# Four of sixteen state drives made with tokens on partitions by ScalarE and turned by TensorE

## Chip, cores and metric
The kernel runs on one core of one Trainium2 chip. The metric is the device time of one execution in microseconds (us), the median of several runs.

## The reference
The input is `x` (4 images, 64 channels, 32x32 positions; so 4 sequences of 1024 tokens). First comes a Mamba block in two directions over the tokens, forward and backward. For one direction and one image, with 128 inner channels and 16 states:

```
xp, z = x @ W_in                       # 128 channels each
xc    = silu(xprev * conv_w0 + xp * conv_w1 + conv_b)
dt_r, Bc, Cc = xc @ W_x                # 8, 16 and 16 columns
dt    = softplus(dt_r @ W_dt + b_dt)
h_s   = exp(dt * A_s) * h_s + (dt * xc) * B_s       # per state s, over the tokens
y     = sum over s of h_s * C_s  +  D * xc
out   = (y * silu(z)) @ W_out
```

The two directions are added, a group norm with silu and the input follow, then causal attention over the tokens and a spectral expert layer. The change touches the Mamba block alone.

## The kernel before
The Mamba stage handles 8 units, u = 0 to 7: image b = u // 2, direction i = u % 2 (0 forward, 1 backward). A tensor of a unit is 128 channels on partitions by 1024 tokens, float32. Every unit goes through its 16 states s in order. The first image is written out, the middle two are a hardware loop, the last is written out. Each engine has its own queue in program order, and semaphores join them.

For a state, four things are made:
- a decay, `exp(dt * A_s)`, by ScalarE (`decay_of`, L734), two states ahead, into one of three SBUF buffers. For states 2, 3, 6, 9, 15 it goes to PSUM instead (`shared_decay_of`, L740): 3, 6, 9 (`WIDE_SHARED`) into `ps_w`, 2 and 15 into `ps_d`;
- a drive, `dtx * B_s`, where `dtx = dt * xc`. B_s is one row of 1024 numbers, spread by a DMA over all 128 partitions into one of four `b_wide` buffers. VectorE makes it into `ps_d` (`drive_step`, L874) for eleven states; GpSimd makes it into SBUF (`share`, L445) for 2, 3, 6, 9, 15, up to three states ahead;
- the scan over the tokens, by VectorE (`scan_step`, L888), into one of four `hidden` buffers;
- the product with C_s by GpSimd (`prod`, L455), and its sum over states in PSUM `ps_y` by TensorE (`sum_states`, L551), three states behind (`Y_LAG`).

In between, the engines prepare the next unit v, in `ps_w`. TensorE: the gate projection (`gate_in`, at s = 2), the conv projection (`conv_in`, s = 3), the low-rank projection (`low_rank`), `dt_in` at s = 10, and matmuls with a unit matrix that add up softplus (`add_rectified`, `add_exponential`, `add_logarithm`). ScalarE: `take_z`, `silu_gate`, `silu_input`, `take_low`, the softplus functions, `take_dt`, `keep_dtx`. `ps_w` passes in turn between these and the decays of states 3, 6 and 9: the decay of 6 waits for `silu_input`, for instance. VectorE makes `dtx` of the next unit in PSUM `ps_x` after scan 14 (`dt_x`, L862), and the gated output of the unit before after scan 1 (`gate_of`, L869). At s = 3 of a forward unit TensorE makes the out product of the image before (`out_product`) and ScalarE takes it (`norm_take`); at s = 3 of a backward unit VectorE ends the group norm's columns and ScalarE applies them (`norm_silu`). `D * xc` is a matmul of `xc` with a diagonal matrix that starts each unit's sum in `ps_y` (`skip_in`, L545).

The SyncE queue issues the B and C loads of each state in turn, each once the buffer's last user is done. In the last unit only state 6 is GpSimd's, and pieces of the attention stage are worked in.

Of the kernel before, what the change touches and what calls it, by code (L numbers as in the profile page):

```python
# [22 lines left out]
ALU = mybir.AluOpType  # L23
# [3 lines left out]
B = 4  # L27
# [5 lines left out]
R = 8  # L33
# [25 lines left out]
POOL_STATES = (2, 3, 6, 9, 15)  # L59
WIDE_SHARED = POOL_STATES[1:4]  # L60
DRIVE_OF = {2: 0, 3: 1, 6: 0, 9: 1, 15: 0}
SHARE = len(POOL_STATES)
SHARE_AHEAD = 3
# [146 lines left out]
def mamba_stage(nc, ins, a, g, e, x1):  # L210
# [6 lines left out]
    with ExitStack() as ctx:  # L217
# [3 lines left out]
        def sem(name):  # L221
# [20 lines left out]
        xc = [sb(f"xc_{d}", [D, L]) for d in DIRS]  # L242
# [7 lines left out]
        rectified = sb("rectified", [D, L])  # L250
        minus_ident = sb("minus_ident", [128, 128])
        skip = [sb(f"skip_{d}", [D, D]) for d in DIRS]
# [5 lines left out]
        b_wide = [sb(f"b_wide_{i}", [D, L]) for i in range(BC_DEEP)]  # L258
# [18 lines left out]
            out_ready a_log_ready one_plus_ready minus_one_ready dt_summed share_ready share_decay diag_ready minus_ready z_kept sum_step tok_psum tok_ready ln_step ln_rstd xn_ready  # L277
# [5 lines left out]
         gated_ready, out_ready, a_log_ready, one_plus_ready, minus_one_ready, dt_summed, share_ready, share_decay, diag_ready, minus_ready, z_kept, sum_step,  # L283
# [5 lines left out]
        b_in = [sem(f"b_in_{i}") for i in range(BC_DEEP)]  # L289
# [8 lines left out]
        LAST_SHARE = POOL_STATES[2:3]  # L298
# [3 lines left out]

        def driven_before(u, s, last=False):
            return (N - SHARE) * u + s - sum(p < s for p in shared(last))

        def shared_before(u, s, last=False):
            return SHARE * u + sum(p < s for p in shared(last))

# [16 lines left out]
        with nc.Block() as block:  # L325

            @block.sync
            def _(sp):
# [39 lines left out]

                def spread(wide, row, done):
                    sp.dma_start(wide[:, :], bass.AP(bc_rows.tensor, row * L, [[0, 128], [1, L]])).then_inc(done, 16)  # L370

                def spread_b(u, i, s):
                    if u or s >= BC_DEEP:
                        drive_done(*divmod(u * N + s - BC_DEEP, N))
                    spread(b_wide[s % BC_DEEP], i * 2 * N + s, b_in[s % BC_DEEP])
# [5 lines left out]
                def unit(u, i):  # L381
                    sp.wait_ge(bc_out, 16 * (u + 1))
                    for s in range(N):
                        spread_b(u, i, s)
# [17 lines left out]
            def _(pool):  # L402
# [38 lines left out]
                def share(u, s):  # L441

                    pool.wait_ge(dtx_kept, u + 1)
                    pool.wait_ge(b_in[s % BC_DEEP], 16 * (u * (N // BC_DEEP) + s // BC_DEEP + 1))
                    nc.gpsimd.tensor_tensor(drive[DRIVE_OF[s]][:, :], dtx[:, :], b_wide[s % BC_DEEP][:, :], ALU.mult).then_inc(share_ready, 1)  # L445

                def batch(b, first=False, last=False):
                    for i in range(2):
                        u = 2 * b + i
                        for s in range(N):  # L450
# [6 lines left out]
                            if s + SHARE_AHEAD in shared(last and i == 1):  # L457
                                share(u, s + SHARE_AHEAD)
                            if s + SHARE_AHEAD - N in shared(last and i == 0) and not (last and i == 1):
                                share(u + 1, s + SHARE_AHEAD - N)  # L460
# [15 lines left out]
                share(0, POOL_STATES[0])  # L476
# [6 lines left out]
            def _(pe):  # L483
# [9 lines left out]
                def gate_in(u, i, b):  # L493

                    pe.wait_ge(dtx_ready, u)
# [8 lines left out]
                def low_rank(u, i):  # L504

                    pe.wait_ge(xc_ready, u + 1)
                    for h, out in enumerate(halves(ps_w)):
                        mm = nc.tensor.matmul(out[0:DT_ROW + R, :], w_x[i], halves(xc[i])[h], start=True, stop=True)
# [9 lines left out]
                def add_part(w, part, start=False, stop=False):  # L518
                    for h, out in enumerate(halves(ps_w)):
                        mm = nc.tensor.matmul(out, w[:, :], halves(part)[h], start=start, stop=stop)  # L520
                    return mm

                def add_rectified(u):

                    pe.wait_ge(abs_ready, u + 1)
                    pe.wait_ge(relu_ready, u)
                    add_part(ident, rectified, start=True)

                def add_exponential(u):

                    pe.wait_ge(exp_ready, u + 2)
                    add_part(ident, soft)

                def add_logarithm(u, i):
# [4 lines left out]
                    add_part(ident, dt[i], stop=True).then_inc(dt_summed, 1)  # L539

                def skip_in(u, i):

                    at_least(pe, gated_ready, u)
# [1561 lines left out]
```

## Time and profile before

| | |
|---|---|
| median of 3 runs | 949.73 us (949.38 to 951.89) |
| span of the profiled execution | 947.3 us |
| from that span to the median | 2.4 us |
| TensorE busy, whole span | 834.3 us, 88% |
| VectorE busy | 710.7 us, 75% |
| GpSimd busy | 549.2 us, 58% |
| ScalarE busy | 508.3 us, 54% |

The profile is one execution. Its span runs from the first to the last instruction; the profiled execution's own time outside the profiler is not listed, so the median stands beside it. Busy shares are over the whole span, though the stages differ: the Mamba stage ends near 482 us, attention near 640 us, and the expert stage, in which TensorE is the busiest, takes the rest. Engines are called PE (TensorE), PEld (its weight loads), DVE (VectorE), ACT (ScalarE), POOL (GpSimd), SP (SyncE).

### The profile page before, as it was taken

What the parts mean: (1) busy time and instruction counts of PE and PEld (TensorE: products, weight loads), DVE (VectorE), ACT (ScalarE), POOL (GpSimd) and SP (SyncE); (2) the same over time, 40 slices, a digit from 0 to 9 for tenths busy, and PEclk for the clock granted to TensorE, in tenths of its full rate; (3) what the DMA queues carried; (4) which work ended last, traced back from release to release, by engine and by line L of the source; (5) the groups of instructions that cost most, each with busy time, mean ns of one, the idle gap of its engine ahead of it and who ended that gap; (6) DMA issues with size and microseconds to landing.
All of it is one profiled execution on the core that took longest, in us unless ns stands there. A gap on an engine that the chain in (4) does not pass through costs nothing. (4 is left out here: it accounts for less than half of the span.)

```text
span 947.3 us, 10224 instructions
## 1 busy us (share of the span) xinstructions
PE 834.3 (88%) x3004; PEld 492.0 (52%) x3004; DVE 710.7 (75%) x767; ACT 508.3 (54%) x702; POOL 549.2 (58%) x373
## 2 busy tenths in 40 slices
PE   5579897979899898986687999989999999999996
PEld 1224342433334333332243555558888888888885
DVE  1999999999999999999965455546565665565664
ACT  4645666556566666643315446456555554555553
POOL 4678989999998998875736955312212211212210
PEclk9799999999999999997987999999999999999999
DMA  7969898889879898796609800002343342343341
GB/s 167 342 201 344 312 332 273 337 311 305 324 257 369 308 327 309 279 328 222 202 0 137 157 0 1 1 1 63 117 133 100 122 133 90 90 133 100 122 118 59
DMA packets 75349, 178.24 MB, mean 188 GB/s; under 512 B 24514, under 2 KB 25044, under 8 KB 75300
## 3 DMA queue, kind: packets, MB, share of 16 engines
q1 hardware_dynamic: 75316, 177.85, 57.9%
q8 instruction: 14, 0.23, 0.1%
q14 instruction: 19, 0.16, 0.1%
HBM read 175.57 MB, written 2.26 MB: 188 GB/s over the span
## 5 line engine op out<-in xcount | busy, mean ns | idle before, releaser
L455 POOL TENSOR_TENSOR prod<-hidden,c_wide 128x1024 f32<-128x1024 f32 x128 | 300.0, 2356 | 64.6 <-DVE hidden L888 60.5
L551 PE MATMUL ps_y<-prod,ident 128*128 128x512 f32 x512 | 244.2, 622 | 27.9 <-POOL prod L455 27.7
L888 DVE TENSOR_TENSOR_SCAN hidden<-decay,ps_d 128x1024 f32<-128x1024 f32 x92 | 209.9, 2281 | 8.3
L1920 PE MATMUL ps_conv<-hankel,u_high 128*128 128x512 f32 (+1 forms) x768 | 215.3, 361 | 0.0
L551 PEld LDWEIGHTS ps_y<-prod,ident 128*128 128x128 f32 x512 | 99.0, 198 | 169.2 <-issue 116.7
L1920 PEld LDWEIGHTS ps_conv<-hankel,u_high 128*128 128x128 f32 x768 | 138.6, 189 | 25.4 <-DVE u_t L1786 0.2
L1920 PE MATMUL ps_conv<-hankel,u_low 128*128 128x512 f32 (+1 forms) x384 | 138.1, 360 | 0.0
L2034 DVE TENSOR_TENSOR stack<-ps_conv,stack 64x512 fp32r<-64x512 f32 x128 | 88.2, 689 | 62.7 <-ACT stack L2001 60.2
L1751 POOL CAST block_mix<-even 128x256 fp32r (+1 forms) x32 | 12.7, 396 | 209.3 <-PE sums L1792 209.3
L2034 DVE TENSOR_TENSOR qk<-ps_conv,qk 64x512 fp32r<-64x512 f32 x128 | 88.2, 689 | 50.2 <-ACT qk L2001 47.5
L874 DVE TENSOR_TENSOR ps_d<-ps_x,b_wide 128x1024 f32<-128x1024 f32 x92 | 113.3, 1232 | 4.9 <-DMA b_wide<-bc_rows 0.4
L2001 ACT ACTIVATE stack<-ps_conv 64x512 fp32r<-64x512 f32 x128 | 75.9, 593 | 75.0 <-PE ps_conv L1920 73.1
L2001 ACT ACTIVATE qk<-ps_conv 64x512 fp32r<-64x512 f32 x128 | 75.9, 593 | 63.3 <-PE ps_conv L1920 61.3
L445 POOL TENSOR_TENSOR drive<-dtx,b_wide 128x1024 f32<-128x1024 f32 x36 | 84.9, 2357 | 6.4 <-ACT dtx L729 6.4
L1920 PEld LDWEIGHTS ps_conv<-hankel,u_low 128*128 128x128 f32 x384 | 72.8, 190 | 13.8
L734 ACT ACTIVATE decay<-dt_b,a_neg_b 128x1024 f32<-128x1024 f32 x48 | 53.2, 1140 | 35.9 <-DVE hidden L888 35.5
L888 DVE TENSOR_TENSOR_SCAN hidden<-ps_w,drive 128x1024 f32<-128x1024 f32 x22 | 50.1, 2279 | 0.0
L734 ACT ACTIVATE decay<-dt_f,a_neg_f 128x1024 f32<-128x1024 f32 x44 | 48.2, 1137 | 2.0 <-DVE dt_f L852 0.9
L1472 DVE TENSOR_REDUCE max_parts<-sums 128x1 f32<-128x512 f32 (+1 forms) x48 | 27.4, 597 | 24.8 <-PE sums L1147 15.2
L1060 POOL TENSOR_TENSOR small<-small,minus_half 128x8 f32<-128x8 f32 x4 | 6.6, 1644 | 55.0 <-DVE small L1442 55.0
L1340 ACT ACTIVATE probs<-ps_t 128x512 f32<-128x512 f32 (+1 forms) x48 | 24.8, 521 | 22.6 <-PE ps_o L1192 22.2
L1792 PE MATMUL sums<-stack,block_mix 128*128 128x512 f32 (+1 forms) x160 | 32.5, 349 | 2.1 <-DVE stack L2034 2.1
(283 smaller groups left out, 1158.8 us busy)
## 6 DMA issues: line engine op xcount, KB each, us to landing
b_wide<-bc_rows SPq DMA_DIRECT2D x128, 512.0 KB, 5.6
c_wide<-bc_rows SPq DMA_DIRECT2D x128, 512.0 KB, 5.2
hankel<-filters SPq DMA_DIRECT2D x32, 1026.0 KB, 5.2
plus<-in_M_phi_plus SPq DMA_DIRECT2D x2, 1024.0 KB, 13.5
minus<-in_M_phi_minus SPq DMA_DIRECT2D x2, 1024.0 KB, 18.9
x_pair<-in_x SPq DMA_DIRECT2D x2, 768.0 KB, 8.5
bc_rows<-mixed_and_low SPq DMA_DIRECT2D x8, 128.0 KB, 5.4
out<-plus SPq DMA_DIRECT2D x4, 256.0 KB, 4.9
```

The source lines that it names most:

```text
L445: nc.gpsimd.tensor_tensor(drive[DRIVE_OF[s]][:, :], dtx[:, :], b_wide[s % BC_DEEP][:, :], ALU.mult).then_inc(share_ready, 1)
L455: nc.gpsimd.tensor_tensor(prod[k % PAIR][:, :], hidden[k % DEEP][:, :], c_wide[s % BC_DEEP][:, :], ALU.mult).then_inc(prod_ready, 1)
L551: mm = nc.tensor.matmul(out, ident[:, :], halves(prod[k % PAIR])[h], start=False, stop=(k % N == N - 1))
L734: nc.scalar.activation(decay[decay_slot(s, last)][:, :], dt[i][:, :], ACT.Exp, scale=a_neg[i][:, s:s + 1]).then_inc(decay_ready, 1)
L874: nc.vector.tensor_tensor(ps_d[:, :], ps_x[:, :], b_wide[s % BC_DEEP][:, :], ALU.mult).then_inc(drive_ready, 1)
L888: nc.vector.tensor_tensor_scan(hidden[k % DEEP][:, order], left[:, order], right[:, order], 0.0, ALU.mult, ALU.add).then_inc(hidden_ready, 1)
L1340: nc.scalar.activation(probs[n % 2][:, 0:hi - lo], ps_t[n % 2][:, 0:hi - lo], ACT.Exp).then_inc(probs_ready, 1)
L1472: nc.vector.tensor_reduce(max_parts[:, i, at // H:at // H + 1], ps_s[c % 2][:, 0:n], AX.X, ALU.max, negate=True).then_inc(part_ready, 1)
L1792: return nc.tensor.matmul(dst, w_block, data, start=first, stop=True, skip_group_check=True)
L1920: mm = nc.tensor.matmul(out, pairs[q][wp][:, 2 * delta + source, :], rows, start=(delta == 0 and term == 0), stop=(delta == 2 * half + 1 a ...
L2001: nc.scalar.activation(stacks[slot][0:C, source, b, :, half * 2 * HEAD:(half + 1) * 2 * HEAD], ps_conv[source][lanes(b), half, :, :], ACT. ...
L2034: nc.vector.tensor_tensor(low, ps_conv[source][lanes(b), half, :, :], high.bitcast(F32), ALU.subtract).then_inc(conv_low, 1)
```

## The change
- GpSimd keeps the drives of states 3, 6, 9 and 15.
- States 2, 4, 7 and 10 (`TURNED_STATES`; in the last unit 2 and 7) get their drive in another layout. At the end of the unit before, TensorE turns `dtx` and the B and C rows, so that tokens stand on partitions (`turn_dtx`: eight turns of 128x128 and eight of 64x128, in three steps through `ps_w`), and ScalarE takes them to `dtx_t` and `b_t` (`take_turned`). In that layout B_s is one number per partition, so ScalarE makes the drive with eight copies of 128 columns, each scaled by a column of `b_t` (`scale_drive`). TensorE turns the eight pieces back into `ps_d` (`turn_drive`), and the scan reads them there.
- The decays of turned states are ordinary ones in SBUF; state 2's was in `ps_d`.
- B is spread over partitions for 12 states of a unit instead of 16, into three buffers instead of four.
- `D * xc` is a scaled ScalarE copy into `ps_y` at s = 3 (`skip_in`), behind `norm_take` or `norm_silu`; TensorE's sum of state 0 waits for it. `xc` has one buffer instead of two.
- ScalarE writes softplus's relu back into `ps_w` instead of to SBUF, and TensorE's `add_rectified` is gone.

```diff
+TURNED_STATES = (2, 4, 7, 10)
+B_DEEP = 3
@@ TensorE
-                def skip_in(u, i):
-                    at_least(pe, gated_ready, u)
-                    for h, out in enumerate(halves(ps_y)):
-                        nc.tensor.matmul(out, skip[i][:, :], halves(xc[i])[h], start=True, stop=False)
+                def turn_dtx(u):
+                    def turn(half):
+                        for t in range(half * SPANS, (half + 1) * SPANS):
+                            mm = nc.tensor.transpose(ps_w[:, t * 128:(t + 1) * 128], dtx[:, t * 128:(t + 1) * 128], ident[:, :])
+                        mm.then_inc(dtx_turned, 1)
+                    pe.wait_ge(dtx_kept, u + 1)
+                    turn(1)
+                    for t in range(TILES):
+                        mm = nc.tensor.transpose(ps_w[:, t * C:(t + 1) * C], dt_low[BC_ROW:, t * 128:(t + 1) * 128],
+                                                 ident[BC_ROW:, BC_ROW:])
+                    mm.then_inc(dtx_turned, 1)
+                    pe.wait_ge(dtx_t_ready, 3 * u + 2)
+                    turn(0)
+
+                def turn_drive(u, s, last=False):
+                    scanned(u, s - (2 if s - 1 in WIDE_SHARED else 1))
+                    for half in range(2):
+                        pe.wait_ge(drive_t_ready, 2 * turned_before(u, s, last) + half + 1)
+                        for t in range(half * SPANS, (half + 1) * SPANS):
+                            mm = nc.tensor.transpose(ps_d[:, t * 128:(t + 1) * 128], drive_t[turned_slot(s, last)][:, t, :], ident[:, :])
+                    mm.then_inc(drive_turned, 1)
...
                             if s == Y_LAG:
+                                turn_drive(u, Y_LAG - 1, not ahead)
                                 if i == 0 and not first:
                                     out_product(b - 1)
+                                if Y_LAG + 1 in turned(not ahead):
+                                    turn_drive(u, Y_LAG + 1, not ahead)
+                                if i == 0 and not first:
                                     conv_in(v, j, bv)
-                                    pe.wait_ge(g.mixed_ready, b)
-                                skip_in(u, i)
...
-                                sum_states(n - Y_LAG, (k - Y_LAG) % (2 * N))
+                                sum_states(n - Y_LAG, (k - Y_LAG) % (2 * N), u if s == Y_LAG else None)
+                            if s > Y_LAG and s + 1 in turned(not ahead):
+                                turn_drive(u, s + 1, not ahead)
...
-                                if s == 11:
-                                    add_rectified(v)
+                                if s == N - 1:
+                                    turn_dtx(v)
@@ ScalarE
+                def skip_in(u, i, taken=0):
+                    at_least(act, gated_ready, u)
+                    at_least(act, g.mixed_ready, taken)
+                    nc.scalar.activation(ps_y[:, :], xc[:, :], ACT.Copy, scale=cols[i][:, 1:2]).then_inc(skip_ready, 1)
...
+                def take_turned(u):
+                    def take(n, half):
+                        act.wait_ge(dtx_turned, 3 * u + n + 1)
+                        nc.scalar.activation(dtx_t[:, half * SPANS:(half + 1) * SPANS, :].rearrange("p t d -> p (t d)"),
+                                             ps_w[:, half * H:(half + 1) * H], ACT.Copy).then_inc(dtx_t_ready, 1)
+                    at_least(act, drive_turned, TURNED * u)
+                    take(0, 1)
+                    act.wait_ge(dtx_turned, 3 * u + 2)
+                    nc.scalar.activation(b_t[:, :, :], ps_w[:, 0:H].rearrange("p (t c) -> p t c", c=C)[:, :, 0:N],
+                                         ACT.Copy).then_inc(dtx_t_ready, 1)
+                    take(2, 0)
+
+                def scale_drive(u, s, last=False):
+                    act.wait_ge(dtx_t_ready, 3 * u + 3)
+                    at_least(act, drive_turned, turned_before(u, s, last) - 1)
+                    for t in range(TILES):
+                        part = nc.scalar.activation(drive_t[turned_slot(s, last)][:, t, :], dtx_t[:, t, :], ACT.Copy, scale=b_t[:, t, s:s + 1])
+                        if t % SPANS == SPANS - 1:
+                            part.then_inc(drive_t_ready, 1)
...
+                            if s == 0 and not final:
+                                scale_drive(u, TURNED_STATES[1])
...
+                            if t in turned(final)[2 - final:]:
+                                scale_drive(u, t, final)
...
+                                skip_in(u, i, taken=b if i == 0 else 0)
                                 silu_input(v, j)
...
                             if s == N - 1:
-                                shared_decay_of(u, i, POOL_STATES[4], hidden_ready, u * N + POOL_STATES[4])
+                                shared_decay_of(u, i, POOL_STATES[3], hidden_ready, u * N + POOL_STATES[3])
                                 keep_dtx(v)
                                 decay_of(v, j, 1, last and i == 0)
+                                take_turned(v)
+                                scale_drive(v, TURNED_STATES[0], last and i == 0)
@@ VectorE
-                            if s in shared(final) and s in WIDE_SHARED:
-                                drive_step(u, s + 1, final)
-                            elif s not in shared(final) and not (s - 1 in shared(final) and s - 1 in WIDE_SHARED):
-                                drive_step(u, s, final)
+                            if s not in shared(final) + turned(final):
+                                drive_step(b, i, s, last)
                             scan_step(u, i, s, final)
```

In this extract `t` in ScalarE's loop is `s + 2`; before `scale_drive` of states 7 and 10 stands the decay of the same state.

## Rows read from the trace of the kernel before

**Rows 1.** The page's head and its busy time by engine, whole span.
```profile
span 947.3 us, 10224 instructions
PE 834.3 (88%) x3004; PEld 492.0 (52%) x3004; DVE 710.7 (75%) x767; ACT 508.3 (54%) x702; POOL 549.2 (58%) x373
```

**Rows 2.** Windows: stretch, length, busy time by engine, clock, DMA share, GB/s.
```profile
193.00:247.00 54.00, 46.98 (x103) 19.25 (x102) 52.19 (x33) 33.08 (x32) 51.28 (x23) 0.97 0.89 308
...
210.20:213.50 3.30, 3.30 (x4) 1.32 (x5) 3.23 (x4) 1.24 (x1) 3.30 (x2) 0.50 1.01 370
```

**Rows 3.** Groups on VectorE, 85 to 409 us: count, busy, mean ns, idle before.
```profile
L888 DVE TENSOR_TENSOR_SCAN hidden<-decay,ps_d 128x1024 f32<-128x1024 f32 x66 | 150.5, 2280 | 5.4
L874 DVE TENSOR_TENSOR ps_d<-ps_x,b_wide 128x1024 f32<-128x1024 f32 x66 | 81.3, 1232 | 4.1 <-DMA b_wide<-bc_rows 0.4
```

**Rows 4.** Timeline of VectorE, unit 3 (backward): start us, length us, idle before.
```profile
192.00 1.21 DVE L862 TENSOR_TENSOR ps_x<-ps_w,xc_b 128x1024 f32<-128x1024 f32 x1
...
202.90 1.20 DVE L869 TENSOR_TENSOR gated_f<-ps_y,gate_f 128x1024 f32<-128x1024 f32 x1
...
207.73 2.28 DVE L888 TENSOR_TENSOR_SCAN hidden<-ps_w,drive 128x1024 f32<-128x1024 f32 x1
209.93 0.18 DVE L178 TENSOR_SCALAR gn<-gn,gn_cols 64x1 f32<-64x1 f32 x1
...
217.67 2.28 DVE L888 TENSOR_TENSOR_SCAN hidden<-ps_w,drive 128x1024 f32<-128x1024 f32 x1
...
246.15 1.21 DVE L862 TENSOR_TENSOR ps_x<-ps_w,xc_f 128x1024 f32<-128x1024 f32 x1
```

**Rows 5.** Timeline of ScalarE, unit 3.
```profile
193.32 1.02 ACT L729 ACTIVATE dtx<-ps_x 128x1024 f32<-128x1024 f32 x1
...
201.78 1.02 ACT L672 ACTIVATE z_raw<-ps_w 128x1024 f32<-128x1024 f32 x1 [5.37 <-PE ps_w L486]
...
206.26 1.28 ACT L684 ACT_TABLE_LOAD   x1
...
210.62 1.24 ACT L186 ACTIVATE mixed_and_low<-mixed_and_low,gn 64x1024 f32<-64x1024 f32 x1 [2.01 <-DVE gn L180]
213.78 1.11 ACT L678 ACTIVATE xc_f<-ps_w,packed_inner_f 128x1024 f32<-128x1024 f32 x1 [1.91 <-PE ps_w L486]
...
216.21 1.12 ACT L740 ACTIVATE ps_w<-dt_b,a_neg_b 128x1024 f32<-128x1024 f32 x1
```

**Rows 6.** Timeline of TensorE, unit 3.
```profile
199.86 1.88 PE L486 MATMUL ps_w<-x_pair,packed_in_f 128*128 x4
...
210.06 3.68 PE L486 MATMUL ps_w<-x_pair,w_conv_f 128*128 x4 [2.21 <-DVE hidden L888]
213.58 7.03 PE L551 MATMUL ps_y<-prod,ident 128*128 128x512 f32 x16
```

**Rows 7.** ScalarE's small copies: a group on the timeline, and a group of the table.
```profile
576.54 2.01 ACT L1302 ACTIVATE u_all<-cen,small 128x64 f32<-128x64 f32 x8
...
L831 ACT ACTIVATE ident_r<-ident 128x128 fp32r<-128x128 f32 x1 | 0.3, 301 | 0.0
```

**Rows 8.** TensorE's turns by a unit matrix, on the timeline.
```profile
416.47 1.17 PE L610 MATMUL ps_w<-ident,x 64*128 64x64 f32 x8
...
447.60 1.92 PE L619 MATMUL ps_w<-ident,late 128*64 128x128 f32 x8 [0.68 <-DVE late L898]
...
617.32 1.04 PE L1772 MATMUL sums<-ident,u_all 128*128 128x128 f32 x8
```

**Rows 9.** DMA issues: KB each, median us from issue to landing.
```profile
b_wide<-bc_rows SPq DMA_DIRECT2D x128, 512.0 KB, 5.6
```

**Rows 10.** Timeline of ScalarE and VectorE, unit 0, and of VectorE, unit 7.
```profile
27.65 1.02 ACT L729 ACTIVATE dtx<-ps_x 128x1024 f32<-128x1024 f32 x1 [0.29 <-DVE ps_d L874]
...
36.30 2.29 DVE L888 TENSOR_TENSOR_SCAN hidden<-ps_d,drive 128x1024 f32<-128x1024 f32 x1 [1.19 <-ACT ps_d L740]
...
420.53 1.22 DVE L874 TENSOR_TENSOR ps_d<-ps_x,b_wide 128x1024 f32<-128x1024 f32 x1
```

More of the change, by code:

```diff
@@ L249, in mamba_stage @@
         soft = sb("soft", [D, L])
[L250 removed]
+        dtx_t = sb("dtx_t", [128, TILES, D])
+        drive_t = [sb(f"drive_t_{i}", [128, TILES, D]) for i in range(2)]
+        b_t = sb("b_t", [128, TILES, N])
         minus_ident = sb("minus_ident", [128, 128])
[L252 removed]
         one_plus = a.late[:, 0:L]
@@ L297, in mamba_stage, with turned, decayed_before @@
         AHEAD = 2
-        LAST_SHARE = POOL_STATES[2:3]
+        LAST_SHARE = (6,)
+        LAST_TURNED = (2, 7)
         def shared(last):
             return LAST_SHARE if last else POOL_STATES
+        def turned(last):
+            return LAST_TURNED if last else TURNED_STATES
         def driven_before(u, s, last=False):
+            return (N - SHARE - TURNED) * u + s - sum(p < s for p in shared(last) + turned(last))
+        def decayed_before(u, s, last=False):
             return (N - SHARE) * u + s - sum(p < s for p in shared(last))
@@ L307, in shared_before, with turned_before, spread_order, b_slot @@
             return SHARE * u + sum(p < s for p in shared(last))
+        def turned_before(u, s, last=False):
+            return TURNED * u + sum(p < s for p in turned(last))
+        def spread_order(last):
+            return [(i, s) for i in range(2) for s in range(N) if s not in turned(last and i == 1)]
+        UNIT_LOADS = N - TURNED
+        def b_slot(i, s, last):
+            return spread_order(last).index((i, s)) % B_DEEP
+        def b_loads(b, i, s, last):
+            return 16 * (2 * UNIT_LOADS // B_DEEP * b + spread_order(last).index((i, s)) // B_DEEP + 1)
+        def turned_slot(s, last):
+            return turned(last).index(s) % 2
         def own_states(last):
@@ L383, in unit @@
                     for s in range(N):
-                        spread_b(u, i, s)
+                        if s not in turned(u == 2 * B - 1):
+                            spread_b(u, i, s)
                         if u or s:
@@ L439, in residual, with share @@
                                             ALU.add).then_inc(g.x1_ready, 1)
[L441 to L445, printed above, removed]
+                def share(b, i, s, last=False):
+                    slot = b_slot(i, s, last)
+                    pool.wait_ge(dtx_kept, 2 * b + i + 1)
+                    pool.wait_ge(b_in[slot], b_loads(b, i, s, last))
+                    nc.gpsimd.tensor_tensor(drive[DRIVE_OF[s]][:, :], dtx[:, :], b_wide[slot][:, :], ALU.mult).then_inc(share_ready, 1)
                 def batch(b, first=False, last=False):
@@ L553, in sum_states @@
+                def sum_states(n, k, seeded=None):
+                    pe.wait_ge(prod_ready, n + 1)
+                    if seeded is not None:
+                        pe.wait_ge(skip_ready, seeded + 1)
+                    for h, out in enumerate(halves(ps_y)):
+                        mm = nc.tensor.matmul(out, ident[:, :], halves(prod[k % PAIR])[h], start=False, stop=True,
+                                              skip_group_check=True)
                     mm.then_inc(prod_summed, 1)
```

95 lines of the change are left out of this document (48 added, 47 removed).

## The prediction
> **What bounds the kernel now.** I read the busy line first [rows 1]: over the whole span TensorE is busiest, but that mixes stages. The windows by unit come next [rows 2]: in one unit of 54 us VectorE is busy 52.2, GpSimd 51.3, TensorE 47.0, ScalarE 33.1. The table of VectorE's groups [rows 3] shows why: 66 own drives of 1.23 us and 96 scans of 2.28 us in six units, with 5.4 and 4.1 us of idle time in all, mostly the 0.1 us between a drive and its scan. So from about 28 us to 482 us VectorE's queue is the time. A unit lasts from one `dt_x` to the next, 192.00 to 246.15 = 54.15 us [rows 4]. TensorE, ScalarE and GpSimd run beside it with waits that cost nothing. What follows the Mamba stage is untouched.
>
> The question is therefore two sums per unit: what leaves VectorE's queue, and whether what ScalarE and TensorE must now deliver arrives before VectorE asks.
>
> **What leaves VectorE.** Eleven own drives per unit become eight; 4, 7 and 10 go. These three stood before a scan of a GpSimd state, where a drive costs its own 1.23 us without the 0.1 us gap: 3 x 1.23 = 3.7 us per unit. State 2 had a GpSimd drive, so it saves VectorE nothing and gives GpSimd one product less, which hides. In the last unit states 2 and 7 lose drives: 1.33 (the row at 420.53 and its gap to the scan) + 1.2 = 2.5 us [rows 10]. Were all of the rest covered: 7 x 3.7 + 2.5 = 28 us less.
>
> **What is added, and its price.**
> A turned drive is eight ScalarE copies of 128 columns with a scale read from SBUF. The trace has eight such copies of 64 columns, 2.01 us as a group, so 0.24 us pitch; and an unscaled copy of 128 columns, 0.30 us alone [rows 7]. The other 64 columns are at most 0.07 us (a 1024-column decay takes 1.12 [rows 5]). I take 0.29 us each, 2.35 us per state, with 2.0 and 2.4 as ends. Four states: 9.4 us. Taking the turned `dtx` and B: two halves and a small copy, 1.4 us. The skip product moves from TensorE to ScalarE, 1.0 us. ScalarE: 33.1 + 11.8 = 45 of some 54 us, in strict order.
> Eight 128x128 turns take 1.04 us as a group in the expert stage (0.11 us pitch), and 1.92 us elsewhere, which I read as the lower clock [rows 8]. I take 0.9 us of queue and 0.2 us until the result is seen. 48 turns per unit, the eight small B turns at 1.17 us, are 5.4 us; the skip and the `rectified` product (4 matmuls each at 0.43 us pitch, 16 in 7.03 us [rows 6]) give back 3.4. TensorE ends near 49 of 54, also in order.
> B has three buffers instead of four: VectorE needs a new B load 3 uses later, three or more drives and scans, over 9 us, against 5.6 us to land [rows 9]; with 28 wide loads instead of 32 per unit I cost it at nothing. If it were late it would show as up to 1 or 2 us at drives 11 to 14.
>
> **A backward unit, by the clock of its own queues.** T = 0 is the end of scan 14 of the unit before (192.0 in [rows 4, 5]).
> 1. ScalarE: decay of 15, `dtx` copy to 2.3 [rows 5], decay 1 to 3.3. TensorE now waits for that copy in `turn_dtx`; sums 13 and 14 stand behind it. Turns 2.4 to 3.9; ScalarE takes them by 4.3; second half of the turns 4.8; ScalarE done 5.5, scale of 2 to 8.0.
> 2. TensorE: sums 13, 14, 15 and the gate projection at 1.72 us each: 4.8 to 11.65, where it ended near 9.6 before. Turn of state 2: 12.5, visible 12.7. VectorE asks after scan 1 and `gate_of`, 12.2 (192.0 to 204.1). Stall 0.5.
> 3. Scan 2 to 15.0, scan 3 to 17.2, the three group-norm steps (from 209.93, 0.2 us each [rows 4]) to 17.8. ScalarE meanwhile: scale of 4 to 10.35, decays 2 and 4, z, decay 3, decay 5, table load (1.28), gate silu: 17.85. Before it idled 5.37 us ahead of z [rows 5]; that cover is used up.
> 4. Now the new serial chain: group-norm silu 1.25 -> 19.1; skip into `ps_y` 1.0 -> 20.1; TensorE's sum 0, which waits for the skip, 1.72 -> 21.9; the conv projection, which for backward units stands behind sum 0, -> 23.6; input silu (1.1), table load (1.28), decay 6 (1.1) with semaphore gaps -> 27.3. VectorE has only scan 4, drive 5 and scan 5 to do: it asks for scan 6 at 23.75. Stall 3.6. Before, the conv ran at 210.06 in parallel with that silu, and decay 6 (216.21 to 217.33) met scan 6 at 217.67 [rows 4 to 6], 0.3 us to spare with one more drive in the way.
> 5. ScalarE: decay 7, scale of 7 -> 30.7; turned and visible 31.3; scan 7 is wanted at 29.55. Stall 1.75. Then decay 8, the low-rank copy, decays 9 and 10, scale of 10 -> 40.3, visible 40.9; wanted 39.5. Stall 1.4.
> Sum: 0.5 + 3.6 + 1.75 + 1.4 = 7.3 of stalls less 3.7: +3.7 us with rounding. Units 3 and 5. Unit 1 has no group norm: +3.2.
>
> **A forward unit.** The out product (8 matmuls, 3.4 us) lies between the turns of 2 and 4, but conv comes before sum 0. Skip is done at 20.0; silu 21.2, decay 6 at 23.55: stall 0.5. TensorE then has sums 0 to 3 (20.1 to 27.0) before the turn of 7, visible 28.05; wanted 25.85: stall 2.2. State 10 is in time. With 0.5 at state 2: 3.2 of stalls less 3.7: -0.4 us. Units 2, 4, 6.
>
> **First and last unit.** Unit 0: the turns and scales begin only after the first `dtx` copy (28.65), and the scales of 2 and of 4 precede decay 2 on ScalarE: 28.7 + turns and takes 4.4 + 2 x 2.35 + 1.05 = 38.9 against a scan of state 2 at 36.30 [rows 10]: +2.7; later stalls of 7 and 10 about 1.7, the rest of the saving 2.4: +2.0. Unit 7: -2.5; there decay 6 does not hang on an input silu.
>
> **The clock.** At 210.06 the conv needs 3.68 us for its four matmuls, where the gate projection took 1.88, after TensorE was idle 2.21 us; the granted clock of that stretch is 0.5, the level of 1.2 GHz [rows 2, 6]. In step 4 TensorE is idle from 15.9 to 20.2 in backward units, so I count half of sum 0 and the conv at that level: +1.7 us in each of three: +5.1.
>
> **Sum.** 2.0 + 3.2 - 1.2 + 7.4 - 2.5 + 5.1 = +14.0 us. The profiled execution's span is 947.3 us; the median of the runs, 949.73, lies 2.4 above it. 947.3 + 14.0 + 2.4 = 963.7 us.
>
> **The rivals.**
> - *All covered* (faster). ScalarE's extra work fits its idle time (33 of 54 us busy) and TensorE keeps its lag of three states: -28 us, 922. For it: every added piece is small against the average idle time. Against: steps 3 and 4 consume the one long idle stretch ahead of z. Halfway, with the backward chain real but turns of 7 and 10 in time, about 945. Chance 0.22 in all below -0.3%.
> - *A draw*: scales at 2.0 us and no clock loss take 3 x 1.2 + 5.1 off the sum, +5, and a little more luck gives within 0.3%. Chance 0.10.
> - *TensorE slow at each unit's start* (slower still). It waits about 2.3 us for `dtx`, then has only turns until 4.8; if the clock falls there, turns cost 1.92 per eight and sums 13 to 15 run partly at 3.68 instead of 1.88: +2.7 us before the turn of state 2, which has no slack, in seven units: +19, 982. For it: 2.21 us of idle time did that at 210.06. Against: at full clock eight turns among matmuls took 1.04 us [rows 8]. Chance 0.18. The Trainium skill, "TensorE: Matmul & The Clock Gate", section "Part 4: PE-mode transpose", goes further: transposes don't count as busy for the clock as matmuls do, so a stretch of turns would not bring it back. No row here shows that or excludes it; by it the time would be this rival's.
> - *Forecast*: 952.6 to 975, chance 0.50.
>
> Faster by over 0.3% 0.22, within 0.3% (2.8 us, about what this kernel's measurement tells from no change) 0.10, slower 0.68. Range 938 to 984: it leaves out the fully covered case and little above.
>
> **What would show it.** VectorE's busy time per unit falls by 3.7 while its idle time grows by more. Scan 6 of backward units waits for ScalarE's decay into `ps_w`, by 3 to 5 us; scan 7 for TensorE's turns in all units, about 2 us. Odd units are about 4 us longer than even ones. ScalarE shows no long wait ahead of z. If scans 6 and 7 start without a wait, steps 4 and 5 are wrong and the time falls toward 922; if scan 2 waits over 2 us everywhere, the third rival holds; waits of VectorE for `b_wide` would make the three buffers the cost.

## The result and the profile after

The changed kernel takes 980.43 us (median of 4 runs, 977.03 to 982.30) against 950.81 us for the kernel before in the same session: ratio 1.0305, 95% interval 1.0272 to 1.0338. The profiled span went from 947.3 to 980.1 us, +32.8. The forecast was +14.0: the direction and most places were right, the size less than half. 980 is close to the third rival (982), but in part by luck: its place, the start of a unit, cost about 10 us more than forecast, not 19, and smaller misses elsewhere make up the rest.

The busy line of the page after answers to [rows 1]. VectorE has 26 us less to do, TensorE and ScalarE more.

```profile
span 980.1 us, 11112 instructions
PE 855.2 (87%) x3312; PEld 524.5 (54%) x3312; DVE 684.7 (70%) x742; ACT 597.6 (61%) x974; POOL 534.5 (55%) x366
```

The waits of VectorE in the Mamba stage (who waited at which line, for whom: us in total, times, longest) are the result in a few lines. L984 is the scan, L961 the gated output; L593 are the turns of drives, L823 the decays into `ps_w`, L602 the sums.

```profile
DVE hidden L984 <- PE ps_d L593: 28.6, 20, 2.2
DVE hidden L984 <- ACT ps_w L823: 19.4, 6, 6.9
DVE hidden L984 <- ACT decay L817: 5.0, 1, 5.0
DVE gated_f L961 <- PE ps_y L602: 4.4, 3, 2.0
...
DVE ps_d L967 <- DMA b_wide<-bc_rows: 2.9, 3, 1.2
DVE gated_b L961 <- PE ps_y L602: 2.8, 3, 1.5
```

They sum to 63 us. Less the 28 us of drives saved and the 3.1 us that VectorE waited there before, 32 remain. Two waits of before also grew (softplus in unit 0, 3.5 instead of 3.1, and the token norm in unit 7, 1.9 instead of 0.6), which makes 33.7 where 32.8 were lost. The third line is scan 2 of unit 0, the line with `b_wide` the waits for a B load. 1.5 of the last line is no loss: the last unit's gated product, behind all scans, waited as long before.

The windows of unit 3 (backward, 62 us), of unit 2 (forward) and of two stretches in unit 3, in the form of [rows 2]:

```profile
203.00:265.00 62.00, 50.56 (x139) 23.56 (x140) 48.45 (x30) 44.35 (x68) 50.08 (x22) 0.89 0.70 238
206.10:209.30 3.20, 2.97 (x7) 1.92 (x8) 3.17 (x2) 1.89 (x7) 2.65 (x2) 0.50 1.01 323
219.70:229.80 10.10, 6.17 (x8) 2.52 (x8) 7.31 (x7) 3.52 (x4) 8.16 (x4) 0.50 0.63 212
147.00:202.00 55.00, 52.01 (x150) 23.36 (x148) 48.69 (x29) 45.89 (x70) 45.14 (x21) 0.97 0.72 266
```

These windows don't begin and end with a unit. Over whole units VectorE was busy 49.1 us in unit 3 instead of 52.3, 3.2 less. What counts is the unit's length without its waits: 50.2 us in unit 3 instead of 54.15, and on average over units 1 to 6 it is 3.8 us less, the 3.7 of the forecast. ScalarE has 44 to 46 us (forecast 45). No engine is full, yet the units are longer. TensorE was granted half its clock in the two short stretches. Where unit 3 loses is on VectorE's timeline (compare [rows 4]; scan 14 of unit 2 ends at 202.3):

```profile
202.24 1.21 DVE L954 TENSOR_TENSOR ps_x<-ps_w,xc 128x1024 f32<-128x1024 f32 x1
...
213.66 1.22 DVE L961 TENSOR_TENSOR gated_f<-ps_y,gate_f 128x1024 f32<-128x1024 f32 x1 [0.53 <-PE ps_y L602]
216.25 2.29 DVE L984 TENSOR_TENSOR_SCAN hidden<-decay,ps_d 128x1024 f32<-128x1024 f32 x1 [1.37 <-PE ps_d L593]
...
234.11 2.29 DVE L984 TENSOR_TENSOR_SCAN hidden<-ps_w,drive 128x1024 f32<-128x1024 f32 x1 [6.86 <-ACT ps_w L823]
238.18 2.29 DVE L984 TENSOR_TENSOR_SCAN hidden<-decay,ps_d 128x1024 f32<-128x1024 f32 x1 [1.77 <-PE ps_d L593]
...
248.12 2.29 DVE L984 TENSOR_TENSOR_SCAN hidden<-decay,ps_d 128x1024 f32<-128x1024 f32 x1 [1.89 <-PE ps_d L593]
```

These are scans 2, 6, 7 and 10. TensorE and ScalarE in the same stretch (answers to [rows 5, 6]):

```profile
204.64 0.65 PE L575 MATMUL ps_w<-ident,dtx 128*128 128x128 f32 x4 [2.65 <-ACT dtx L789]
...
207.24 6.38 PE L602 MATMUL ps_y<-prod,ident 128*128 128x512 f32 x12
213.46 1.88 PE L521 MATMUL ps_w<-x_pair,packed_in_f 128*128 x4
215.18 1.03 PE L593 MATMUL ps_d<-ident,drive_t 128*128 128x128 f32 x8
218.68 1.11 PE L593 MATMUL ps_d<-ident,drive_t 128*128 128x128 f32 x8 [2.47 <-DVE hidden L984]
223.72 3.75 PE L602 MATMUL ps_y<-prod,ident 128*128 128x512 f32 x4 [3.93 <-ACT ps_y L738]
227.27 3.17 PE L521 MATMUL ps_w<-x_pair,w_conv_f 128*128 x4
```
```profile
208.19 4.78 ACT L810 ACTIVATE drive_t<-dtx_t,b_t 128x128 f32<-128x128 f32 x16
...
221.33 1.24 ACT L189 ACTIVATE mixed_and_low<-mixed_and_low,gn 64x1024 f32<-64x1024 f32 x1 [0.34 <-DVE gn L183]
222.48 1.10 ACT L738 ACTIVATE ps_y<-xc,packed_inner_b 128x1024 f32<-128x1024 f32 x1
230.48 1.11 ACT L732 ACTIVATE xc<-ps_w,packed_inner_f 128x1024 f32<-128x1024 f32 x1 [6.90 <-PE ps_w L521]
231.61 1.28 ACT L882 ACT_TABLE_LOAD   x1
232.90 1.12 ACT L823 ACTIVATE ps_w<-dt_b,a_neg_b 128x1024 f32<-128x1024 f32 x1
```

Read it as one chain: group-norm silu, skip, sum 0, conv, input silu, table load, decay 6, scan 6, 221.3 to 234.1, and nothing of it overlaps. Sum 0 and the conv take 6.6 us at the lower clock level; at the upper they took 3.5 (e8 below).

Unit by unit (from the end of scan 14 to the next one's), in us:

| unit | before | after | difference | forecast |
|---|---|---|---|---|
| 0 (from the start) | 84.6 | 88.0 | +3.4 | +2.0 |
| 1 (backward) | 53.5 | 58.95 | +5.5 | +4.9 |
| 2 | 54.0 | 55.35 | +1.4 | -0.4 |
| 3 (backward) | 54.15 | 62.6 | +8.5 | +5.4 |
| 4 | 53.9 | 54.7 | +0.8 | -0.4 |
| 5 (backward) | 54.15 | 62.7 | +8.6 | +5.4 |
| 6 | 54.2 | 55.9 | +1.7 | -0.4 |
| 7 | 70.0 | 71.7 | +1.8 | -2.5 |
| rest of the program | 468.8 | 470.0 | +1.2 | 0 |

The starts of the units tell the rest. TensorE turns `dtx` there and then makes sums 13 to 15, whose end the gated product and the turn of state 2 wait for. In us, for the changed kernel:

| unit | time at the lower clock level at its start | sums 13 to 15 take | wait at gated product and scan 2 |
|---|---|---|---|
| 1 | none | 5.3 | 0.4 |
| 2 | 3.4 | 7.0 | 2.0 |
| 3 | 3.4 | 6.4 | 1.9 |
| 4 | none | 5.4 | 0.6 |
| 5 | 6.8 | 7.0 | 3.4 |
| 6 | 3.4 | 7.0 | 2.05 |
| 7 | 6.8 | 7.8 | 2.9 |

The forecast was a wait of 0.5 in units 1 to 6 and none in unit 7. Where the clock stayed up it came out so.

### The profile page after: what moved, and what is told of

Same layout as the page of the kernel before. It is cut to its first block and busy times, and to the rows that moved or that the text cites. A ratio compares the mean times of both kernels' runs of the same rounds, so it can differ in the third digit from the quotient of the medians.

```text
span 980.1 us, 11112 instructions
## 1 busy us (share of the span) xinstructions
PE 855.2 (87%) x3312; PEld 524.5 (54%) x3312; DVE 684.7 (70%) x742; ACT 597.6 (61%) x974; POOL 534.5 (55%) x366
## 5 line engine op out<-in xcount | busy, mean ns | idle before, releaser
L602 PE MATMUL ps_y<-prod,ident 128*128 128x512 f32 x512 | 252.4, 640 | 28.7 <-ACT ps_y L738 21.9
L984 DVE TENSOR_TENSOR_SCAN hidden<-decay,ps_d 128x1024 f32<-128x1024 f32 x99 | 226.3, 2286 | 40.0 <-PE ps_d L593 28.6
L602 PEld LDWEIGHTS ps_y<-prod,ident 128*128 128x128 f32 x512 | 101.5, 206 | 157.9 <-issue 128.3
L2126 DVE TENSOR_TENSOR stack<-ps_conv,stack 64x512 fp32r<-64x512 f32 x128 | 88.2, 689 | 62.7 <-ACT stack L2093 60.2
L1843 POOL CAST block_mix<-even 128x256 fp32r (+1 forms) x32 | 12.7, 397 | 209.4 <-PE sums L1884 209.4
L2126 DVE TENSOR_TENSOR qk<-ps_conv,qk 64x512 fp32r<-64x512 f32 x128 | 88.2, 689 | 50.2 <-ACT qk L2093 47.5
L967 DVE TENSOR_TENSOR ps_d<-ps_x,b_wide 128x1024 f32<-128x1024 f32 x69 | 85.0, 1232 | 6.6 <-DMA b_wide<-bc_rows 2.9
L817 ACT ACTIVATE decay<-dt_b,a_neg_b 128x1024 f32<-128x1024 f32 x51 | 57.2, 1139 | 29.4 <-DVE hidden L984 29.0
L810 ACT ACTIVATE drive_t<-dtx_t,b_t 128x128 f32<-128x128 f32 x240 | 72.4, 387 | 0.6
L481 POOL TENSOR_TENSOR drive<-dtx,b_wide 128x1024 f32<-128x1024 f32 x29 | 68.3, 2356 | 2.9 <-DMA b_wide<-bc_rows 2.9
L984 DVE TENSOR_TENSOR_SCAN hidden<-ps_w,drive 128x1024 f32<-128x1024 f32 x22 | 50.1, 2276 | 19.6 <-ACT ps_w L823 19.4
L593 PE MATMUL ps_d<-ident,drive_t 128*128 128x128 f32 x240 | 36.3, 290 | 29.1 <-DVE hidden L984 18.0
L593 PEld LDWEIGHTS ps_d<-ident,drive_t 128*128 128x128 f32 x240 | 28.1, 147 | 49.6 <-issue 20.7
L817 ACT ACTIVATE decay<-dt_f,a_neg_f 128x1024 f32<-128x1024 f32 x48 | 53.4, 1137 | 1.3 <-DVE dt_f L944 0.9
```

The source lines that it names most:

```text
L593: mm = nc.tensor.transpose(ps_d[:, t * 128:(t + 1) * 128], drive_t[turned_slot(s, last)][:, t, :], ident[:, :])
L602: mm = nc.tensor.matmul(out, ident[:, :], halves(prod[k % PAIR])[h], start=False, stop=True, skip_group_check=True)
L810: part = nc.scalar.activation(drive_t[turned_slot(s, last)][:, t, :], dtx_t[:, t, :], ACT.Copy, scale=b_t[:, t, s:s + 1])
L817: nc.scalar.activation(decay[decay_slot(s, last)][:, :], dt[i][:, :], ACT.Exp, scale=a_neg[i][:, s:s + 1]).then_inc(decay_ready, 1)
L967: nc.vector.tensor_tensor(ps_d[:, :], ps_x[:, :], b_wide[slot][:, :], ALU.mult).then_inc(drive_ready, 1)
L984: nc.vector.tensor_tensor_scan(hidden[k % DEEP][:, order], left[:, order], right[:, order], 0.0, ALU.mult, ALU.add).then_inc(hidden_ready, 1)
```

## The experiments

A is the theory that particular waits at particular places of in-order queues cost the time; B that the engines' amount of added work does, wherever it stands; C the clock; D the sums behind the turns of `dtx`. Ratios are to the kernel before, with 95% intervals; the changed kernel stands at 1.0305. Waits are VectorE's.

**e1_conv_first: the conv ahead of sum 0 in all units.**
```diff
-                                if i == 0 and not first:
+                                if ahead:
                                     conv_in(v, j, bv)
...
-                                if s == Y_LAG and (i == 1 or first):
-                                    conv_in(v, j, bv)
```


> The changed kernel (980.4 us), but in every unit TensorE's conv projection stands ahead of the sum of state 0, as it does in forward units; so it no longer waits for the skip copy. Theory A, the serial chain of backward units (group-norm silu, skip, sum 0, conv, input silu, table load, decay 6): the wait of scan 6 falls from 6.9 us to at most 1 in units 3 and 5 and from 5.1 to about 0 in unit 1, less some 0.4 us at scan 7: 16 to 18 us less, 962 to 965 us. Rival B, the amount of ScalarE's work is the cost whatever the order: the wait moves on to the turned states 7 and 10, and at most 5 us go. Rival C, TensorE at 1.2 GHz makes the chain long: the conv still takes 3.2 us or more after an idle stretch, but off the chain; the saving is that of theory A, and what is left of it is the wait for conv, 1 to 2 us per backward unit.

Measured: 964.84 us, 1.0147 (1.0094 to 1.0200). Scan 6 waits 1.0 us in unit 3 instead of 6.9, in unit 5 0.9 instead of 5.5, in unit 1 1.7 instead of 5.1.
```profile
DVE hidden L982 <- PE ps_d L593: 27.3, 19, 3.0
...
DVE hidden L982 <- ACT ps_w L821: 5.7, 6, 1.7
```
That is theory A's size, with nothing left out, but its place only in part. Units 1, 3 and 5 got 10.2 us shorter together, not 16 to 18, since 1.0 to 1.1 us came back at scan 7 of units 1 and 3 and 1.5 at scan 13 of unit 3. Unit 0, whose conv had also stood behind sum 0, gave 4.1. Unit 6 gave 1.6, and there the edit changes nothing in the order of the queues. Only the clock differs:
```profile
386.91 7.00 PE L602 MATMUL ps_y<-prod,ident 128*128 128x512 f32 x12
396.63 2.29 DVE L984 TENSOR_TENSOR_SCAN hidden<-decay,ps_d 128x1024 f32<-128x1024 f32 x1 [1.46 <-PE ps_d L593]
```
```profile
371.33 5.32 PE L602 MATMUL ps_y<-prod,ident 128*128 128x512 f32 x12
379.37 2.29 DVE L982 TENSOR_TENSOR_SCAN hidden<-decay,ps_d 128x1024 f32<-128x1024 f32 x1 [0.47 <-PE ps_d L593]
```
The first two lines are TensorE's sums and scan 2 in unit 6 of the changed kernel (clock 0.50 from 386.9 to 389.9), the last two the same in unit 6 of e1 (clock 1.00 from 369.7 to 372.7). Sums 13 to 15 took 7.0 and 5.3 us; scan 2 waited 1.5 and 0.5, the gated product 0.6 and nothing. In unit 3 of e1 the conv still ran at the lower level (3.78 us for 4 matmuls) and left 1.0 us of wait at scan 6, as C expected.

**e2_skip_first: ScalarE's skip copy ahead of the group-norm silu.**
```diff
-                                if not first:
-                                    if i == 0:
-                                        norm_take(b - 1)
-                                    else:
-                                        norm_silu(nc, act, g, b - 1)
+                                if i == 0 and not first:
+                                    norm_take(b - 1)
                                 skip_in(u, i, taken=b if i == 0 else 0)
+                                if i == 1 and not first:
+                                    norm_silu(nc, act, g, b - 1)
```


> The changed kernel with ScalarE's skip copy ahead of the group-norm silu in backward units, the conv still behind sum 0. Theory A: the chain loses the wait for VectorE's group-norm steps and the silu, about 1.7 us in units 3 and 5, more where TensorE's shorter idle stretch keeps its clock: 3 to 8 us less in all, 972 to 977 us. Rival B: nothing is left out, so no change (980).

Measured: 975.47, 1.0262 (1.0209 to 1.0314). The intervals overlap, so the times alone don't show a gain; in the trace scan 6 of units 3 and 5 waits 4.4 and 4.6 us instead of 6.9 and 5.5, as A expected. 1.5 us of what the profiled run gained is unit 6 again, where the clock stayed up as in e1.

**e3_two_scales: two scaled copies per turned drive instead of eight.**
```diff
-                    for t in range(TILES): ... ACT.Copy, scale=b_t[:, t, s:s + 1]   # 128 columns
+                    for h in range(2): ... ACT.Copy, scale=b_t[:, lo, s:s + 1]      # 512 columns
```


> The changed kernel with each turned drive made by two ScalarE copies of 512 columns instead of eight of 128 (the B of the first token tile of each half stands for all four, so the drives are not the true ones): ScalarE saves about 1.2 us per turned state, 4.8 per unit. Rival B, ScalarE's load is the cost: 4 to 4.8 us per unit less, 28 to 34 in all, 947 to 952 us. Theory A: the chain of states 3 to 6 hangs on scan 3 and on TensorE; only scans 7 and 10 of backward units (1.2 us each), unit 0 (2.4) and a little in forward units gain: 8 to 12 us less, 968 to 972 us.

Measured: 960.09, 1.0102 (1.0050 to 1.0155), 19 us less: between the two, and both sizes missed. Scan 6 waits 5.1 and 5.6 us in units 1 and 5, as long as before, and 5.3 instead of 6.9 in unit 3, so that chain hardly hangs on the scales; scans 7 and 10 of backward units wait 0.6 to 0.8 each instead of 1.7 to 1.9, the waits for `b_wide` are gone, unit 0 gains 5 us, and the last unit lost its waits at state 2. ScalarE's amount counts at more places than I had listed, two thirds of the loss in all, but it is not the whole.

**e5_conv_sum13: e1, and sum 13 ahead of the turns of dtx.**
```diff
-                            if not (first and k < Y_LAG):
+                            if not (first and k < Y_LAG) and s != 0:
...
                                 if s == N - 1:
+                                    sum_states(n + 1 - Y_LAG, (k + 1 - Y_LAG) % (2 * N))
                                     turn_dtx(v)
```


> The kernel of e1 and besides TensorE's sum of state 13 ahead of the turns of dtx, in the 2.7 us in which it waits for the dtx copy. Theory D, the wait of scan 2 and of the gated product comes from sums 13 to 15 standing behind the turns: up to 1.7 us less in each of seven units beside e1's gain, 8 to 11 in all: 952 to 956 us. Rival C, the clock at a unit's start is what delays: with the idle stretch cut from 2.7 to 1 us it stays at 2.4 GHz there, and up to 1.7 us more go in the units in which it had fallen. Rival B: no more than e1.

Measured: 958.06, 1.0073 (1.0048 to 1.0097), a little above the 952 to 956 of D; the intervals of e1 and e5 touch, the profiled spans are 962.8 and 953.9. Where e1 had 4.4 and 2.1 us of waits for the gated product's sums (L959) and 0.4 to 1.4 us at scan 2 in each of units 1 to 7, e5 has only the 1.5 behind the last scan, which the kernel before has too, and at scan 2 0.7 us in unit 5 and under 0.2 elsewhere:
```profile
DVE hidden L983 <- PE ps_d L593: 21.6, 17, 3.0
...
DVE gated_b L960 <- PE ps_y L602: 1.5, 1, 1.5
```
And the clock no longer fell at the start of any unit; in the changed kernel it had in units 2, 3, 5, 6 and 7. D and C both hold here, and this run does not part them. The traces of the runs that keep the turns ahead of sums 13 to 15 do (the changed kernel, e1, e2, e3, e6, e7, e8 and e11): in units whose start kept the upper level the two waits make at most 0.6 us, and in those where the clock fell they make 1.2 to 3.4. So D, the mere place of the sums, is worth about the 0.5 that I had forecast, and what lies above it is the clock.

**e6_scales_early: scales of 7 (backward units) and 10 moved into ScalarE's idle stretches.**
```diff
-                            if t in turned(final)[2 - final:]:
+                            if t in turned(final)[2 - final:] and (final or t == 7 and i == 0):
                                 scale_drive(u, t, final)
+                            if s == 7 and not final:
+                                scale_drive(u, TURNED_STATES[3])
...
+                                if i == 1:
+                                    scale_drive(u, TURNED_STATES[2])
                                 silu_input(v, j)
```


> The changed kernel with ScalarE's scales moved into its idle stretches and nothing left out: state 7's (backward units) ahead of the input silu, where ScalarE waits 6.9 us for the conv, state 10's ahead of the low-rank copy. Theory A (order, not amount): scan 10's wait in backward units (1.7 to 1.9 us) goes, scan 7's (1.8) falls to about 0.4, unit 0 gains a little; scan 7 in forward units (2.1 us) stays, as TensorE's sums stand ahead of that turn: 10 to 12 us less than 980, about 969. Rival B (amount): the saved time comes back at another wait of ScalarE, at most 3 us less.

Measured: 965.11, 1.0158 (1.0130 to 1.0185), 14 us less; the waits at scan 10 are gone, backward scan 7 waits at most 0.2 us, forward scan 7 stays at 2.1. The same work at another place in the queue: A, a little more than expected.

**e7_turn_first: turns of 7 and 10 ahead of the sum in their slot.**
```diff
+                            if s > Y_LAG and s + 1 in turned(not ahead):
+                                turn_drive(u, s + 1, not ahead)
                             if not (first and k < Y_LAG):
                                 sum_states(n - Y_LAG, (k - Y_LAG) % (2 * N), u if s == Y_LAG else None)
-                            if s > Y_LAG and s + 1 in turned(not ahead):
-                                turn_drive(u, s + 1, not ahead)
```


> The changed kernel with the turns of states 7 and 10 ahead of the sum in their slot instead of behind it. Theory A: scan 7 in forward units waits for TensorE's queue alone, so its wait falls from 2.1 us to about 0.4; in backward units ScalarE's scale ends last and nothing changes: 5 us less, 975. Rival B: no change, or the later sums delay the softplus chain and the time grows.

Measured: 1002.90, 1.0548 (1.0513 to 1.0582), 23 us more. I expected less time, and was wrong. TensorE's queue in unit 3:
```profile
244.14 0.66 PE L593 MATMUL ps_d<-ident,drive_t 128*128 128x128 f32 x4 [2.44 <-ACT drive_t L810]
245.31 0.66 PE L593 MATMUL ps_d<-ident,drive_t 128*128 128x128 f32 x4 [0.51 <-ACT drive_t L810]
245.80 3.60 PE L602 MATMUL ps_y<-prod,ident 128*128 128x512 f32 x8
249.24 1.88 PE L543 MATMUL ps_w<-xc,packed_inner_f 128*104 128x512 f32 x4
...
255.80 0.66 PE L593 MATMUL ps_d<-ident,drive_t 128*128 128x128 f32 x4 [2.97 <-ACT drive_t L810]
```
The turn waits 3 us for ScalarE, and now the sum and the low-rank projection stand behind that wait; decay 9 and softplus get late, and scans 9 and 13 wait too (1.6 and 2.8 us in unit 3). I had asked who waits for the turn, and not what stands behind it.

**e8_fill: extra matmuls in TensorE's idle stretch of units 3 and 5.**
```diff
+                                if fills: fill(u, 2)      # 2 x 2 halves into ps_y
                                 turn_drive(u, Y_LAG + 1, not ahead)
+                                if fills: fill(u, 2).then_inc(filled, 1)
```


> The changed kernel with eight extra matmuls (4 before and 4 behind the turn of state 4, their result written over by the skip copy) in TensorE's idle stretch of units 3 and 5; nothing else moves. Theory C (clock): sum 0 and the conv then run at 2.4 GHz, 3.5 us together instead of 6.6 in unit 3 and about 5 in unit 5, and scan 6 waits 3.6 us in both: 3 to 6 us less than 980. Rival (the clock does not depend on that idle stretch, or the chain is not what scan 6 waits for): no change, or slower by the extra matmuls.

Measured: 979.71, 1.0316 (1.0288 to 1.0344): no difference in time, where C had expected 3 to 6 us less. The trace parts two effects:
```profile
219.25 3.60 PE L611 MATMUL ps_y<-dtx,ident 128*128 128x512 f32 x8
224.15 1.96 PE L602 MATMUL ps_y<-prod,ident 128*128 128x512 f32 x4 [1.30 <-ACT ps_y L752]
225.94 1.88 PE L521 MATMUL ps_w<-x_pair,w_conv_f 128*128 x4
```
Sum 0 and the conv take 3.5 us instead of 6.6: the idle stretch had cost the clock, 3.1 us in unit 3. But the fill was twice what I had counted (each matmul call shows as two in the trace, 16 in all instead of 8) and held the skip back by 1.75 us (end of the skip 23.0 us after scan 14 instead of 21.25). Scan 6 still waits 5.4 us. Less those 1.75 that is 3.6, an estimate of the chain without the clock's part, and it is the stall that step 4 had.

**e9_all and e10_order: e10 has the edits of e1, e2, e5 and e6 together; e9 has e7's besides and the one below.**
```diff
                             if t < N and t not in shared(final):
                                 decay_of(u, i, t, final)
+                            if s == 0 and not final:
+                                scale_drive(u, TURNED_STATES[1])     # was ahead of decay_of
```


> All moves together, nothing left out: conv ahead of sum 0, skip ahead of the group-norm silu, sum 13 ahead of the turns of dtx, scales of 7 and 10 in ScalarE's idle stretches, turns ahead of the sums, decay 2 ahead of the scale of 4. Theory A: what is left is the saving of 28 us less the waits that no move removes (scan 2 in unit 0 about 3 us, scan 6 about 1 us in each unit, some 0.5 us at scans 7 and 10): 12 to 20 us under the kernel before, 930 to 938 us, ratio 0.98 to 0.987. Rival B (ScalarE's and TensorE's amount of work is the bound): it stays above 950.

> e9 without its two moves that e7 and unit 0 speak against: turns of 7 and 10 again behind the sum of their slot, decay 2 again behind the scale of 4. Kept: conv ahead of sum 0, skip ahead of the group-norm silu, sum 13 ahead of the turns of dtx, scales of 7 and 10 in ScalarE's idle stretches. Theory A (each wait has its own place in a queue): e5's units with the waits of scans 7 and 10 in backward units gone, 13 us under e5: 941 to 946 us, ratio 0.989 to 0.995. Rival B (the engines' amount of work is the bound and waits only move): no better than e9, 950 to 956.

Measured: e9 952.92, 1.0032 (1.0012 to 1.0051); e10 951.16, 1.0021 (0.9997 to 1.0045). Both give back nearly all of the 3%, and neither beats the kernel before; my 12 to 20 us under it, and then 941 to 946, were too low. e10's waits:
```profile
DVE hidden L986 <- ACT ps_w L822: 12.6, 9, 2.6
DVE hidden L986 <- PE ps_d L593: 11.9, 10, 2.2
...
DVE hidden L986 <- ACT decay L816: 7.2, 3, 5.0
```
Scan 6 waits 0.9 to 2.6 us in each of units 1 to 6, against at most 1.7 in e1: work that moves ahead of the input silu seems to come back here, the part of B that holds; no run has that move alone with the conv first. In e10's profiled run the clock also fell at the starts of units 3, 5 and 7, though sum 13 stood ahead of the turns; the gated product and scan 2 waited 1.95 us in unit 3 and 2.8 in unit 5.

**e11_skip_pe and e12_order_skip_pe: the skip product on TensorE again, in the changed kernel and in e10.**
```diff
+                            if s == Y_LAG:
+                                skip_in(u, i, ...)     # matmul with skip[i], ahead of sum 0
```


> The changed kernel with one part undone: the skip product is TensorE's matmul with a diagonal again, in its old place ahead of sum 0; all else as changed. Theory A: in backward units sum 0 no longer waits for the group-norm silu and ScalarE's copy; skip, sum 0 and conv follow the turn of state 4 at once, the conv ends about 4 to 5 us earlier in units 3 and 5 and 3 in unit 1, and the idle stretch that costs the clock is gone: 10 to 14 us less than 980, 966 to 970. Rival B: ScalarE has 1 us less and TensorE 1.7 us more per unit; forward units get 1.7 us longer at scan 7, and the total stays within 5 us of 980.

> e10 with the skip product on TensorE. Theory A: with the conv first, the skip is off the chain on either engine; on TensorE it adds 1.7 us ahead of the turn of 7, which in forward units is the last: 5 us more than e10. Rival B (ScalarE's amount): 7 us less than e10.

Measured: e11 972.60, 1.0236 (1.0191 to 1.0282); e12 963.17, 1.0150 (1.0105 to 1.0196). Undoing the skip's move gives 7 us back, not 10 to 14: backward units gain 2.8 to 5 us (unit 3: 59.0 instead of 62.6) and forward ones lose 0.5 to 1.3. With the conv first, the skip on TensorE costs 12 us, more than the 5 that A expected and against B's 7 less: it is then right on ScalarE, and it was its place in the chain that hurt.

**e13_order_two_scales: e10 with e3's two copies.**
```diff
-                    for t in range(TILES): ...   # e10: eight copies of 128 columns
+                    for h in range(2): ...       # two of 512
```


> e10 with each turned drive made by two ScalarE copies of 512 columns, as in e3 (the drives are not the true ones): 4.8 us of ScalarE's time per unit less on top of the better order. Rival B (ScalarE's amount is the bound): 28 to 34 us less than e10's 951, about 920. Theory A: what e10 still waits for is partly ScalarE (scan 6, 1 to 2.6 us per unit, and unit 0) and partly TensorE's queue ahead of the turn of 7 in forward units (2.1 us), which stays: 10 to 16 us less, 935 to 941, ratio 0.985 to 0.992.

Measured: 938.65, 0.9876 (0.9828 to 0.9924). 12.5 us less than e10, in A's range, far from B's 28 to 34. Like e3 it leaves work out (the B values of three token tiles in four), so it is no version to use; it shows what the small copies cost once the order is right. What stays is mostly the turn of 7:
```profile
DVE hidden L987 <- PE ps_d L593: 16.9, 11, 3.7
...
DVE hidden L987 <- ACT ps_w L823: 2.7, 2, 1.7
```

## Where the prediction was right, and which step failed

- *What leaves VectorE*: 3.7 us per unit was right (3.6 to 3.9 in units 1 to 6, length less waits). Unit 7's 2.5 did not come: state 2 there waited for TensorE (1.9 us at the gated product, 1.0 at the scan), and the drive saved at state 7 only uncovered a wait for GpSimd's step of the token norm, 1.9 us instead of 0.6.
- *Prices*: a turned drive is 2.43 us on ScalarE (2.35 forecast) and 1.03 us on TensorE (1.04 from [rows 8]). Right.
- *Step 4*, the serial chain: right in place and mechanism (e1, e2, e8). With the clock term it gave 5.3 us at scan 6 of units 3 and 5; measured 6.9 and 5.5.
- *Step 5*, scans 7 and 10: 1.75, 2.2 and 1.4 forecast; 1.8, 2.1 and 1.9 measured.
- *Step 2 failed.* "Turn of state 2: 12.5, visible 12.7 ... Stall 0.5" priced sums 13 to 15 at 1.72 us each, the upper clock level. That held in units 1 and 4 alone (waits of 0.4 and 0.6 us). In units 2, 3, 5, 6 and 7 the clock fell 2 to 5 us after the unit's start, sums 13 to 15 took 6.4 to 7.8 us instead of 5.3 to 5.4, and the gated product, a wait that I had put at zero, and scan 2 waited 1.9 to 3.4 us together. In units 1 to 7 the two waits make 13.2 us where the forecast had 3.0 (none in unit 7). This is the mechanism of the third rival, which I had priced at 2.7 us per unit and given 0.18: it came in five of seven units, at 1.4 to 2.9 us. Less 0.5 in each of these five, the clock's part is about 9.7 of the 10.2 us missed, an estimate from these waits.
- *The clock term* of step 4 was half of what unit 3 lost: +1.7 us, where sum 0 and the conv lost 3.1 (e8).
- *B loads*: 2.9 us of waits at drive 11 of units 2, 4 and 6, against my nothing and 0.4 before. The place is where I said late loads would show. That the three buffers are the cause is not shown: four beside the rest of the change were not tried, and in e3 and e13, with three buffers, these waits are gone.
- *Unit 0* was 1.4 us longer than forecast, and the rest of the program 1.2; the second is unexplained.
- Two slips in the working change nothing: 7.3 less 3.7 is 3.6, and the turns at 617 us stand in the attention stage, not in the expert stage.

The misses, in us: state 2 in units 1 to 7 10.2, scan 6 1.1 (18.0 in units 1 to 6, 16.9 forecast), scan 10 in backward units 1.3 (5.5 less 3 x 1.4), the token norm in unit 7 1.3, unit 0 1.4, the rest of the program 1.2, B loads 2.9. That is 19.4 for the 18.8 between +14.0 and +32.8; the drives saved about 0.1 us more per unit than forecast.

## What to carry to other kernels

Work moved to engines with average idle time costs nothing only if it stands at no place where the bound engine's next input is made: follow one period through every in-order queue, and ask of each new wait what is queued behind it. Moving an operation to another engine can join two chains that ran side by side (here group norm and conv); moving one call in TensorE's queue gave back 15 of 30 us with no work removed, and with four such moves the change broke even. And where the forecast prices TensorE's work behind a new wait, take the price at both clock levels: here 5.3 us of sums became up to 7.8.

## What the runs showed of the hardware

Turns of 128x128 float32 come every 0.11 us at TensorE's upper level (eight in 1.03 us) and every 0.21 us at the lower (four in 1.11 us). A ScalarE copy of 128 columns, scaled by a column read from SBUF, takes 0.39 us, and eight in a row 2.43, against 1.10 to 1.12 for the skip's one copy of 1024 columns.

At the starts of units 1 to 7 of the changed kernel TensorE stood idle for 1.5 to 3.2 us and then had turns; the granted clock fell 2 to 5 us after the start in five of them. The length of the idle stretch alone doesn't tell which: it was 1.75 us in units 1 and 2 and 1.5 in units 4 and 6, and the clock fell in 2 and 6. With sum 13 ahead of the turns it fell at no start in e5, and at three in e10, where TensorE had waited 2.2 to 2.4 us for a product of GpSimd's just before. The Trainium skill's "TensorE: Matmul & The Clock Gate", section "Part 4: PE-mode transpose", says that transposes do not count as busy the way matmuls do. No run here shows that or excludes it. In units 1, 2, 4 and 6 of e5 the turns followed sum 13 with no idle time ahead and the clock stayed up, but there are only some 2 us of them, with matmuls on both sides.
